# A 32-batch attention stage: a reordered step, maxima negated in the reduction, queries two batches ahead, and key transfers issued before stores

## The chip, the core and the metric

The kernel runs as one program on one core of a Trainium2 chip. The core has five instruction queues that run side by side and meet only through semaphores: TensorE (PE: matmuls and transposes), VectorE (DVE), ScalarE (ACT), GpSimd (POOL) and SyncE (SP, which here only issues DMA transfers). SBUF is the on-chip memory with 128 partitions; PSUM is the memory that TensorE writes. The metric is the device time of one execution in microseconds (us). The kernel before takes 1517.27 us (median of 3 runs, 1517.0 to 1519.42).

## What is computed

Two transformer layers on x of 32 batches x 128 tokens x 256 features. The change touches only the first piece, a cross attention with 16 heads of 16 features and the layer norm behind it:

```python
def _mha(q, k, v, mask):
    qh = q.reshape(B, S, H, hd).transpose(0, 2, 1, 3)      # kh, vh alike
    scores = jnp.einsum('bhqd,bhkd->bhqk', qh, kh) / jnp.sqrt(jnp.float32(hd))
    scores = scores + mask[:, None, :, :].astype(scores.dtype) * NEG_INF
    probs = jax.nn.softmax(scores, axis=-1)
    out = jnp.einsum('bhqk,bhkd->bhqd', probs, vh)
    return out.transpose(0, 2, 1, 3).reshape(B, S, D)

x1 = x + _mha(layernorm(x), ctx, ctx, mask)
y = layernorm(x1)      # goes into a quantised feed-forward network, then a
                       # second attention and a mixture of 8 experts
```

## The kernel before, in words

`attention0` (lines 44 to 687) runs stage A, the attention above; `feed_forward0` and later functions follow behind a barrier and are not touched. Stage A has no scheduler: every engine's queue is written out by hand as a function `step`, called once for each batch b = 0 to 31 and a few times more to drain. Some calls are unrolled, the middle ones stand in a hardware loop (`Fori`) of four steps; `inside(b, first, last)` leaves out what does not exist at the ends. An engine runs its queue strictly in order, so the order in `step` decides who waits for whom.

For one batch the work is: POOL subtracts the mean and multiplies by the inverse deviation (`queries`, L320 and L323). PE transposes the result (`turn_qy`, L434) and it is scaled out of PSUM into `qT` (`copy_qy`, L639). PE writes mask times -10000 into the score banks (`masks`, L382) and adds the 16 heads' scores (`scores`, L392). The scores fill `ps_score`, four PSUM banks in two halves of 8 heads, and there is only one such tile: the masks of the next batch can go into half 0 only when its exponentials have been read, into half 1 only when DVE's subtraction has read it. DVE takes the row maxima of each half (`maximum`, L507). For half 0 it negates them (`negate`, L511) and ACT uses them as the bias of eight exponentials (`shifted_exponentials`, L619); for half 1 DVE subtracts them itself (`subtract`, L516) and ACT does one exponential over all 8 heads (`exponentials`, L625). PE transposes the probabilities in four quarters through two PSUM buffers (`transposes`, L403), ACT copies each quarter out (`copy_probT`, L631), PE multiplies with the values (`weighted`, L414), ACT copies the sum out (`copy_out`, L648), PE turns it back (`turn_out`, L421), and DVE divides by the sums of the exponentials (`divide`, L522 and L524). POOL adds the result to x (`residual`, L329). DVE takes the statistics (`deviation`, L531), POOL the inverse deviation, DVE normalises and takes the largest absolute value (`normalise`, L540, L543), PE transposes y in the same PSUM tile as the queries (L438), and it is copied to `yT` (L642). DVE also takes the statistics of the batch four ahead (`statistics_ahead`, L571).

SP's `step` waits until x1 of batch b is ready, stores it (L247), and in every second step loads the keys of a pair of batches as 8 transfers (`load_keys`, L214) into one of two slots. In the first step it also issues the last mask chunk (L227), three quarters of the values (`load_v`, L222) and b1T (L261), and late in the stage three groups of weights (`load_w2`, L253).

## Time and profile before

| | |
|---|---|
| runs (3) | 1517.27 us median, 1517.0 to 1519.42 |
| the profiled execution | 1516.37 us, its span 1514.6 us |
| mean granted TensorE clock | 0.954 |
| PE / DVE / ACT / POOL busy, whole span | 89% / 74% / 69% / 25% |
| stage A ends (barrier) | at 292.16 us |
| its busy time in stage A, of 292.16 us | PE 226.69, DVE 212.92, ACT 200.86, POOL 126.72 us |

All later times are from the profiled execution, in us from its span's start. "T of step b" is when DVE begins the first `maximum` of batch b. A start-to-start distance between two neighbouring instructions of an engine is what the first occupies of it; the durations shown are a little longer, since neighbours overlap.

### The profile page before, as it was taken

To read this page: it belongs to the slowest core of one execution; us is meant where nothing else is said; L and a number is where in the kernel's file an instruction comes from. 1 tells how busy PE (TensorE), PEld (TensorE's weight loads), DVE (VectorE), ACT (ScalarE), POOL (GpSimd) and SP (SyncE) were. 2 spreads that over 40 slices of the span, in tenths; PEclk is the share of its full clock that TensorE was granted. 3 is DMA by queue.
4 is the path that set the end of the run, shared out by engine and by line. 5 is a ranking of instruction groups with operands and counts; after the bars stand their busy time and mean duration, and the time that the engine had idled before them with its cause. 6 is when DMAs were issued, how large, how long until landed. Compare 5 with 4: busy or idle time off the path is not lost. (4 is left out here: it accounts for less than half of the span.)

```text
span 1514.6 us, 34646 instructions
## 1 busy us (share of the span) xinstructions
PE 1352.3 (89%) x11261; PEld 1158.5 (76%) x11261; DVE 1126.2 (74%) x1948; ACT 1045.4 (69%) x2717; POOL 374.6 (25%) x639
## 2 busy tenths in 40 slices
PE   5788888899899989997799999899998759999996
PEld 3555555587787768797688888888887649999996
DVE  6677778797858887276577777777776468888895
ACT  4677777566559976562578777777777328888885
POOL 5344444200001111002011111111111124445543
PEclk9999999999899999999799999999999769999999
DMA  7411034448037889733413324233331057211110
GB/s 222 126 35 32 28 101 135 141 163 295 28 125 250 261 289 292 255 112 107 165 64 130 100 79 130 80 101 123 94 135 36 22 196 281 99 55 51 55 43 10
DMA packets 102058, 191.02 MB, mean 126 GB/s; under 512 B 12948, under 2 KB 68145, under 8 KB 95540
## 3 DMA queue, kind: packets, MB, share of 16 engines
q1 hardware_dynamic: 91572, 155.80, 30.5%
q0 software_dynamic: 10176, 33.57, 7.5%
q8 instruction: 67, 1.10, 0.3%
q14 instruction: 51, 0.42, 0.1%
q10 hardware_dynamic: 192, 0.13, 0.0%
HBM read 124.17 MB, written 68.03 MB: 127 GB/s over the span
## 5 line engine op out<-in xcount | busy, mean ns | idle before, releaser
L2040 ACT ACTIVATE c_w_raw<-c_ps_score,c_neg_max 128x128 f32<-128x128 f32 x512 | 182.9, 387 | 51.7 <-DVE c_neg_max L1900 50.9
L2413 PE MATMUL d_ps_hT<-d_zT,d_w_tile 128*128 128x128 f32 x1248 | 147.2, 277 | 2.5 <-DVE d_zT L2520 2.5
L2413 PEld LDWEIGHTS d_ps_hT<-d_zT,d_w_tile 128*128 128x128 f32 x1248 | 144.0, 193 | 3.2 <-DVE d_zT L2520 3.2
L2426 PE MATMUL d_ps_y<-d_w_parts,d_hT 128*128 128x256 f32 x936 | 120.3, 284 | 1.8 <-DVE d_res L2551 1.8
L631 ACT ACTIVATE a_probT<-a_ps_probT 128x512 f32<-128x512 f32 x128 | 71.1, 622 | 68.2 <-PE a_ps_probT L403 68.0
L2586 ACT ACTIVATE d_h<-d_ps_hT,d_b1T 128x128 f32<-128x128 f32 x312 | 88.5, 366 | 41.4 <-PE d_ps_hT L2413 41.4
L2040 ACT ACTIVATION_READ_ACCUMULATOR c_w_raw<-c_ps_score,c_neg_max 128x1 f32 x512 | 116.0, 227 | 0.0
L2426 PEld LDWEIGHTS d_ps_y<-d_w_parts,d_hT 128*128 128x128 f32 x936 | 113.2, 189 | 2.1 <-DVE d_res L2551 2.0
L507 DVE TENSOR_REDUCE a_row_max<-a_ps_score 128x8 f32<-128x1024 f32 x64 | 78.0, 1219 | 44.9 <-PE a_ps_score L392 44.9
L1777 PE MATMUL c_ps_proj<-c_xnT,c_wq 128*128 128x256 f32 x768 | 110.0, 296 | 0.0
L1825 PE MATMUL c_ps_aux<-c_wo,c_attnT 128*128 128x256 f32 x768 | 105.1, 296 | 0.0
L2539 DVE TENSOR_TENSOR d_w_parts<-d_w,d_w_parts 128x1024 fp32r<-128x1024 f32 x78 | 95.3, 1221 | 12.0 <-ACT d_w_parts L2598 12.0
L1777 PEld LDWEIGHTS c_ps_proj<-c_xnT,c_wq 128*128 128x128 f32 x768 | 98.5, 198 | 5.0 <-issue 4.8
L1825 PEld LDWEIGHTS c_ps_aux<-c_wo,c_attnT 128*128 128x128 f32 x768 | 98.4, 198 | 4.3 <-issue 0.4
L1900 DVE TENSOR_REDUCE c_neg_max<-c_ps_score 128x4 f32<-128x512 f32 x128 | 82.5, 686 | 22.5 <-PE c_ps_score L1747 22.5
L1907 DVE TENSOR_TENSOR c_w_raw<-c_w_raw,c_inv_sum 128x512 f32<-128x512 f32 x128 | 88.9, 694 | 4.4
L2598 ACT ACTIVATE d_w_parts<-d_w 128x1024 fp32r x78 | 81.9, 1051 | 10.0 <-PE d_ps_y L2426 10.0
L1144 ACT ACTIVATE b_act<-b_ps 128x512 f32<-128x512 f32 (+1 forms) x96 | 54.5, 603 | 49.7 <-PE b_ps L1039 42.4
L1088 PE MATMUL b_ps<-b_w_parts,b_ctx_high 128*128 128x512 f32 x256 | 82.4, 403 | 4.3 <-DMA b_ctx_low<-split_scratch 4.3
L1078 PE MATMUL b_ps<-b_ctx_high,b_w_parts 128*128 128x512 f32 x256 | 82.5, 397 | 2.8 <-ACT b_out L1207 2.7
L619 ACT ACTIVATE a_prob<-a_ps_score,a_shift 128x128 f32<-128x128 f32 x256 | 75.1, 409 | 11.5 <-DVE a_shift L511 10.4
L1722 POOL TENSOR_TENSOR c_var_o<-c_mv_o,c_eps 128x1 f32<-128x1 f32 x32 | 6.1, 190 | 307.8 <-DVE c_mv_o L1941 307.8
(307 smaller groups left out, 3527.9 us busy)
## 6 DMA issues: line engine op xcount, KB each, us to landing
keys_scratch<-b_out SPq DMA_DIRECT2D x64, 256.0 KB, 3.2
values_scratch<-b_out SPq DMA_DIRECT2D x64, 256.0 KB, 3.9
c_kT<-keys_scratch SPq DMA_DIRECT2D x16, 1024.0 KB, 6.4
d_w<-w_in SPq DMA_DIRECT2D x16, 1024.0 KB, 7.5
split_scratch<-b_split SPq DMA_DIRECT2D x12, 1024.0 KB, 4.7
c_v_more<-values_scratch SPq DMA_DIRECT2D x24, 512.0 KB, 4.1
a_w<-w_in SPq DMA_DIRECT2D x64, 128.0 KB, 2.6
b_ctx_high<-split_scratch POOLq DMA_DIRECT2D x16, 512.0 KB, 5.3
```

The source lines that it names most:

```text
L1078: last = pe.matmul(ps[:, bank(n), :], w_parts[:, h, a, k, column:column + P], ctx_parts[c % 2][b][:, k, :], start=(j == 0), stop=(j == ND ...
L1088: last = pe.matmul(ps[:, bank(n), :], ctx_parts[c % 2][a][:, k, t * P:(t + 1) * P], w_parts[:, h, b, k, :], start=(j == 0), stop=(j == ND ...
L1777: last = pe.matmul(ps_proj[:, j, h * PT:(h + 1) * PT], weights[:, a, k, blk * P:(blk + 1) * P], src[:, c, k, :], start=(n == 0), stop=(n = ...
L1825: last = pe.matmul(ps_aux[:, 0:D], attnT[:, s, a, blk, :], wo[:, c, blk, :], start=False, stop=(n == BLKS * len(PARTS) - 1))
L1900: dve.tensor_reduce(neg_max[:, n, :], ps_score[:, n % 2], AX_X, ALU.max, negate=True).then_inc(max_done, 1)
L1907: dve.tensor_tensor(prob[:, n], prob[:, n], inv_sum[:, n, :].unsqueeze(2).to_broadcast([P, HB, P]), ALU.mult).then_inc(prob_ready, 1)
L2040: last = act.activation(prob[:, n, j, :], ps_score[:, n % 2, j, :], ACT.Exp, bias=neg_max[:, n, j:j + 1], accum_out=row_sum[:, n, j:j + 1])
L2413: last = pe.matmul(ps_hT[:, f, :], w1_tile[:, half, k, n * P:(n + 1) * P], zT[:, s, k, :], start=(k == 0), stop=(k == ND - 1))
L2426: last = pe.matmul(ps_y[:, 0:D], hT[:, s, a, f, :], w2_parts[:, half, b, n, :], start=(f == 0 and (a, b) == PARTS[0]), stop=(f == FB - 1 a ...
L2539: dve.tensor_tensor(w2_parts[:, half, 1], w2[:, e, half * FB // 2:(half + 1) * FB // 2, :], w2_parts[:, half, 0].bitcast(F32), ALU.subtrac ...
L2586: act.activation(h[:, f, :], ps_hT[:, f, :], ACT.Relu, bias=b1T[:, e, f:f + 1]).then_inc(h_ready, 1)
L2598: act.activation(w2_parts[:, half, 0], w2[:, e, half * FB // 2:(half + 1) * FB // 2, :], ACT.Copy)\
```

## The change

No piece of arithmetic is dropped except one small instruction. `negate` goes: the reduction of half 0 gets `negate=half == 0`, and the bias of the exponentials is `row_max` itself. The rest is order:

- PE: a step does masks and scores of b, then the second half of the transposes and all of `weighted` of batch b-2, then queries of b+2 (and y), then the first half of the transposes of b-1, and `turn_out` of b-2 last. Before, all four quarters and `weighted` were of b-1, in the step directly behind.
- DVE: both maxima and the subtraction come first, `divide` behind them. In odd steps DVE makes the two copies of `copy_qy`, which ACT made in every step.
- ACT: exponentials first, the copy of `out` between their two groups, the copies of the transposed probabilities last.
- POOL: queries of b+3 instead of b+2, values of b instead of b+1.
- SP: keys are issued when their scores are done, and x1 is stored two steps later, so the wait for x1 no longer stands ahead of them. The values come in step 1 (one quarter) and step 3 (two), the last mask chunk and b1T in step 1. The groups of `w2` go in steps 22, 24 and 30 instead of 21, 23 and 28.

```diff
+                def store_x1(b):
+                    sp.wait_ge(x1_ready, b + 1)
+                    sp.dma_start(x1_dram[b], x_sb[:, b, :]).then_inc(x1_stored, 16)
+
+
+
                 def step(b, u, pair):
                     if u % 2 == 1 and inside(b, 0, NB - 5):
                         sp.wait_ge(scores_done, b + 1)
                         load_keys(pair + 2, u // 2)
-                    sp.wait_ge(x1_ready, b + 1)
-                    sp.dma_start(x1_dram[b], x_sb[:, b, :]).then_inc(x1_stored, 16)
+                    if inside(b, 2, NB + 1):
+                        store_x1(b - 2)
 
...
-                    if b == 0:
+                    if b == 1:
                         load_mask(3)
-                        for c in range(1, 4):
-                            load_v(c)
                         sp.dma_start(b1T[:], b1T_dram).then_inc(b1_loaded, 16)
+                        load_v(1)
+                    if b == 3:
+                        load_v(2)
+                        load_v(3)
...
                 def step(b, u):
                     s = u % 2
-                    if inside(b, 0, NB - 3):
-                        queries(b + 2, s, (u + 2) % UN)
+                    if inside(b, 0, NB - 4):
+                        queries(b + 3, 1 - s, (u + 3) % UN)
                     if inside(b, 2, NB + 1):
                         residual(b - 2, s)
                         inverse_deviation(b - 2, s)
                     if inside(b, 4, NB - 5):
                         deviation_ahead(b, u)
-                    if inside(b, 1, NB - 2):
-                        values(b + 1, 1 - s)
+                    if inside(b, 2, NB - 1):
+                        values(b, s)
 
                 deviations(0, 2, 1)
                 queries(0, 0, 0)
+                queries(1, 1, 1)
                 masks(0)
-                queries(1, 1, 1)
                 deviations(2, 2, 2)
+                queries(2, 0, 2)
                 pool.wait_ge(v_loaded[0], 16)
...
                 def step(b, u):
-                    p, pu = b - 1, (u - 1) % UN
                     if inside(b, 0, NB - 1):
                         if u == 0 and not isinstance(b, int):
                             pe.wait_ge(mask_ready, 4)
                         masks(b)
                         scores(b, u)
+                    if inside(b, 2, NB + 1):
+                        transposes(b - 2, u % 2, 2)
+                        transposes(b - 2, u % 2, 3)
+                        for q in range(NQ):
+                            weighted(b - 2, (u - 2) % UN, q)
+                    turn_qy(b + 2, u % 2)
                     if inside(b, 1, NB):
-                        transposes(p, pu % 2, 0)
-                        transposes(p, pu % 2, 1)
+                        transposes(b - 1, 1 - u % 2, 0)
+                        transposes(b - 1, 1 - u % 2, 1)
                     if isinstance(b, int) and b == NB:
                         turn_weights(0)
                     if inside(b, 2, NB + 1):
                         turn_out(b - 2)
-                    turn_qy(b + 1, (u + 1) % 2)
-                    if inside(b, 1, NB):
-                        transposes(p, pu % 2, 2)
-                        transposes(p, pu % 2, 3)
-                        for q in range(NQ):
-                            weighted(p, pu, q)
 
...
                 def maximum(b, half):
-                    n = 2 * b + half + 1
                     if half == 0:
                         dve.wait_ge(scores_done, b + 1)
-                    dve.tensor_reduce(row_max[:, half, :], ps_score[:, half], AX_X, ALU.max).then_inc(max_done, 1)
-                    dve.wait_ge(max_done, n)
-
-                def negate(b):
-                    dve.tensor_scalar(shift[:], row_max[:, 0, :], -1.0, None, ALU.mult).then_inc(shift_ready, 1)
+                    dve.tensor_reduce(row_max[:, half, :], ps_score[:, half], AX_X, ALU.max, negate=half == 0).then_inc(max_done, 1)
 
                 def subtract(b, s):
+                    dve.wait_ge(max_done, 2 * (b + 1))
                     if inside(b, 2, NB):
                         dve.wait_ge(probT_done, NQ * (b - 1))
                     dve.tensor_tensor(prob[:, s, 1], ps_score[:, 1],
...
+                def copy_qy(g, s):
+                    dve.wait_ge(qy_done, g + 1)
+                    if inside(g, 0, NB - 1):
+                        if inside(g, 2, NB - 1):
+                            dve.wait_ge(scores_done, g - 1)
+                        dve.tensor_scalar(qT[:, s], ps_qy[:, 0], float(HD0) ** -0.5, None, ALU.mult).then_inc(qT_ready, 1)
+                    if inside(g, 6, NB + 5):
+                        dve.tensor_copy(yT[:, :, bass.ds((g - 6) * P, P)], ps_qy[:, 1]).then_inc(yT_ready, 1)
+
                 def step(b, s):
-                    here = inside(b, 0, NB - 1)
-                    if here:
+                    if inside(b, 0, NB - 1):
                         maximum(b, 0)
-                        negate(b)
+                        maximum(b, 1)
+                        subtract(b, s)
+                    if s == 1:
+                        copy_qy(b + 2, s)
                     if inside(b, 2, NB + 1):
                         divide(b - 2, s)
-                    if here:
-                        maximum(b, 1)
-                        subtract(b, s)
                     if inside(b, 3, NB + 2):
                         normalise(b - 3, 1 - s)
                     if inside(b, 2, NB + 1):
...
                 def shifted_exponentials(b, s, q):
                     if q == 0:
-                        act.wait_ge(shift_ready, b + 1)
+                        act.wait_ge(max_done, 2 * b + 1)
                     for h in range(HB * q, HB * (q + 1)):
-                        last = act.activation(prob[:, s, 0, h, :], ps_score[:, 0, h, :], ACT.Exp, bias=shift[:, h:h + 1])
+                        last = act.activation(prob[:, s, 0, h, :], ps_score[:, 0, h, :], ACT.Exp, bias=row_max[:, 0, h:h + 1])
                     if q == 1:
...
                 def step(b, u):
-                    here, back = inside(b, 0, NB - 1), inside(b, 1, NB)
-                    if back:
-                        copy_probT(b - 1, 0)
-                        copy_probT(b - 1, 1)
+                    here = inside(b, 0, NB - 1)
                     if here:
                         shifted_exponentials(b, u % 2, 0)
-                    copy_qy(b + 1, (u + 1) % 2)
-                    if back:
-                        copy_probT(b - 1, 2)
-                        copy_probT(b - 1, 3)
+                    if inside(b, 2, NB + 1):
+                        copy_out(b - 2)
                     if here:
                         shifted_exponentials(b, u % 2, 1)
                         exponentials(b, u % 2)
-                    if back:
-                        copy_out(b - 1)
+                    if u % 2 == 0:
+                        copy_qy(b + 2, 0)
+                    if inside(b, 1, NB):
+                        for q in range(NQ):
+                            copy_probT(b - 1, q)
 
```


What stands in TensorE's queue for one middle step (batch 6), from its masks to its last instruction:

```order
L382 MATMUL a_ps_score<-a_neg_eye,a_mask 128x512 x4
L392 MATMUL a_ps_score<-a_keys,a_qT 128x256 x8
L403 MATMUL a_ps_probT<-ident,a_prob 128x128 x8
L421 MATMUL a_ps_out<-ident,a_outT 128x128 x4
L434 MATMUL a_ps_qy<-ident,a_q_in 128x128 x2
L438 MATMUL a_ps_qy<-ident,a_y 128x128 x2
L403 MATMUL a_ps_probT<-ident,a_prob 128x128 x8
L414 MATMUL a_ps_out<-a_probT,a_v_ones 32x128 x16
```
and with the change:

```order
L389 MATMUL a_ps_score<-a_neg_eye,a_mask 128x512 x4
L399 MATMUL a_ps_score<-a_keys,a_qT 128x256 x8
L410 MATMUL a_ps_probT<-ident,a_prob 128x128 x8
L421 MATMUL a_ps_out<-a_probT,a_v_ones 32x128 x16
L441 MATMUL a_ps_qy<-ident,a_q_in 128x128 x2
L445 MATMUL a_ps_qy<-ident,a_y 128x128 x2
L410 MATMUL a_ps_probT<-ident,a_prob 128x128 x8
L428 MATMUL a_ps_out<-ident,a_outT 128x128 x4
```
The products with the values (`a_ps_out<-a_probT,a_v_ones`) move from the step's end to right behind the first transposes, and the turn of `a_outT` moves to the step's end.

VectorE's queue, an unrolled step before (batch 3):

```order
L507 TENSOR_REDUCE a_row_max<-a_ps_score 128x8
L511 TENSOR_SCALAR a_shift<-a_row_max 128x8
L522 RECIPROCAL a_inv_sum<-a_ps_out 128x16
L524 TENSOR_TENSOR a_attn<-a_ps_out,a_inv_sum 128x256
L507 TENSOR_REDUCE a_row_max<-a_ps_score 128x8
L516 TENSOR_TENSOR a_prob<-a_ps_score,a_row_max 128x1024
L540 TENSOR_SCALAR a_y<-a_x,a_mv,a_rstd 128x256
L543 TENSOR_REDUCE ymax<-a_y 128x1
L531 BN_STATS a_stats<-a_x 128x6
L534 BN_AGGR a_mv<-a_stats 128x2
```
and with the change, an unrolled odd step (batch 5):

```order
L513 TENSOR_REDUCE a_row_max<-a_ps_score 128x8 x2
L519 TENSOR_TENSOR a_prob<-a_ps_score,a_row_max 128x1024
L555 TENSOR_SCALAR a_qT<-a_ps_qy 128x256
L557 COPY yT<-a_ps_qy 128x2x128
L525 RECIPROCAL a_inv_sum<-a_ps_out 128x16
L527 TENSOR_TENSOR a_attn<-a_ps_out,a_inv_sum 128x256
L543 TENSOR_SCALAR a_y<-a_x,a_mv,a_rstd 128x256
L546 TENSOR_REDUCE ymax<-a_y 128x1
L534 BN_STATS a_stats<-a_x 128x6
L537 BN_AGGR a_mv<-a_stats 128x2
```
`a_shift` is gone, the reciprocal comes behind the subtraction, and two copies out of `a_ps_qy` have come in ahead of it. Even steps do not have these two.

SyncE's queue at the start, from the last part of x on, before:

```order
L218 DMA a_x<-x_in 128x8x256
L247 DMA x_scratch<-a_x 128x256
L227 DMA a_mask_int<-mask_t_in 128x1024
L222 DMA a_v_raw<-ctx_in 128x8x256 x3
L261 DMA b1T<-b1T_in 128x64
L214 DMA a_keys<-ctx_blocks_in 16x2x256 x8
```
and with the change:

```order
L216 DMA a_x<-x_in 128x8x256
L212 DMA a_keys<-ctx_blocks_in 16x2x256 x8
L225 DMA a_mask_int<-mask_t_in 128x1024
L263 DMA b1T<-b1T_in 128x64
L220 DMA a_v_raw<-ctx_in 128x8x256
L242 DMA x_scratch<-a_x 128x256
L212 DMA a_keys<-ctx_blocks_in 16x2x256 x8
L242 DMA x_scratch<-a_x 128x256
L220 DMA a_v_raw<-ctx_in 128x8x256 x2
```
The 8 key transfers stood behind a store (`x_scratch<-a_x`), a mask chunk, three quarters of the values and b1T; now they stand ahead of all of these.

## Rows read from the trace of the kernel before

**Rows 1.** The windows view: span, busy us (instructions) per engine, granted clock, DMA.

```profile
core 0: us, PE busy (x) PEld busy (x) DVE busy (x) ACT busy (x) POOL busy (x), PEclk, DMA share, GB/s
54.22:85.40 31.18, 26.62 (x305) 18.73 (x306) 25.36 (x48) 24.61 (x64) 13.14 (x29) 0.95 0.12 36
85.40:252.94 167.54, 137.51 (x1521) 90.94 (x1522) 130.00 (x240) 123.37 (x320) 74.39 (x162) 0.93 0.23 69
94.91:102.52 7.61, 6.29 (x77) 4.32 (x77) 6.28 (x13) 6.10 (x16) 2.19 (x6) 1.00 0.11 30
102.52:112.03 9.51, 7.94 (x77) 4.95 (x77) 6.60 (x12) 6.21 (x16) 5.22 (x12) 0.82 0.12 34
252.94:275.37 22.43, 18.94 (x229) 12.99 (x230) 17.09 (x31) 18.34 (x48) 8.07 (x17) 1.00 0.18 47
```
**Rows 2.** Waits in stage A: who waited for whom, us in total, times, longest.

```profile
engine line waited for: us in total, times, longest us
...
DVE a_row_max L507 <- PE a_ps_score L392: 44.9, 31, 4.1
...
PE a_ps_score L392 <- DMA a_keys<-ctx_blocks_in: 6.4, 2, 6.1
```
**Rows 3.** The same view for SyncE's queue in stage A.

```profile
SPq L247 <- POOL a_x L329: 122.6, 25, 9.9
```
**Rows 4.** The timeline of one step at full clock, three engines mixed.

```profile
start us, us, engine line op out<-in xcount [idle before <-releaser]
...
208.28 1.22 ACT L619 ACTIVATE a_prob<-a_ps_score,a_shift 128x128 f32<-128x128 f32 x4
...
209.64 1.03 PE L382 MATMUL a_ps_score<-a_neg_eye,a_mask 128*128 128x512 f16 x4 [0.70 <-ACT a_prob L619]
...
211.82 1.22 DVE L507 TENSOR_REDUCE a_row_max<-a_ps_score 128x8 f32<-128x1024 f32 x1 [0.75 <-PE a_ps_score L392]
...
213.08 0.57 DVE L511 TENSOR_SCALAR a_shift<-a_row_max 128x8 f32<-128x8 f32 x1
...
213.56 0.24 DVE L522 RECIPROCAL a_inv_sum<-a_ps_out 128x16 f32<-128x16 f32 x1
213.68 1.14 ACT L619 ACTIVATE a_prob<-a_ps_score,a_shift 128x128 f32<-128x128 f32 x4
213.84 0.42 DVE L524 TENSOR_TENSOR a_attn<-a_ps_out,a_inv_sum 128x256 f32<-128x256 f32 x1
214.18 1.21 DVE L507 TENSOR_REDUCE a_row_max<-a_ps_score 128x8 f32<-128x1024 f32 x1
214.44 0.73 POOL L329 TENSOR_TENSOR a_x<-a_x,a_attn 128x256 f32 x1 [0.82 <-DVE a_attn L524]
...
214.69 0.40 ACT L639 ACTIVATE a_qT<-a_ps_qy 128x256 f32<-128x256 f32 x1
...
215.52 1.23 DVE L516 TENSOR_TENSOR a_prob<-a_ps_score,a_row_max 128x1024 f32<-128x1024 f32 x1
...
216.66 0.41 DVE L540 TENSOR_SCALAR a_y<-a_x,a_mv,a_rstd 128x256 f32 x1
...
217.54 0.42 DVE L531 BATCH_NORM_STATS2 a_stats<-a_x 128x6 f32 x1
...
218.28 0.43 DVE L571 BATCH_NORM_STATS2 a_stats_next<-a_x 128x6 f32 x1
```
**Rows 5.** The same timeline one step earlier: masks, and the maximum that follows.

```profile
200.41 1.89 PE L382 MATMUL a_ps_score<-a_neg_eye,a_mask 128*128 128x512 f16 x4 [0.70 <-ACT a_prob L619]
...
204.21 1.23 DVE L507 TENSOR_REDUCE a_row_max<-a_ps_score 128x8 f32<-128x1024 f32 x1 [2.31 <-PE a_ps_score L392]
```
**Rows 6.** VectorE's timeline: first maxima of batch 1 and batch 4.

```profile
24.91 1.23 DVE L507 TENSOR_REDUCE a_row_max<-a_ps_score 128x8 f32<-128x1024 f32 x1 [2.40 <-PE a_ps_score L392]
...
54.22 1.23 DVE L507 TENSOR_REDUCE a_row_max<-a_ps_score 128x8 f32<-128x1024 f32 x1 [3.63 <-PE a_ps_score L392]
```
**Rows 7.** SyncE's row for the keys of batches 4 and 5.

```profile
43.80 5.31 SPq L214 DMA_DIRECT2D a_keys<-ctx_blocks_in  x8
```
**Rows 8.** TensorE's row for the scores of batch 4.

```profile
52.07 2.09 PE L392 MATMUL a_ps_score<-a_keys,a_qT 32*128 32x256 f32 x16 [6.06 <-DMA a_keys<-ctx_blocks_in]
```
**Rows 9.** SyncE's row for the first group of w2.

```profile
215.66 11.29 SPq L253 DMA_DIRECT2D a_w<-w_in  x24
```
**Rows 10.** TensorE's row for the turn of batch 31's output.

```profile
285.44 0.66 PE L421 MATMUL a_ps_out<-ident,a_outT 128*128 128x128 f32 x4
```

More of the change, by code:

```diff
@@ L264, in _ @@
                         step(UN * i + u, u, 2 * i + u // 2)
-                for b in range(20, NB):
+                for b in range(20, NB + 2):
                     step(b, b % UN, b // 2)
-                    if b == 21:
+                    if b == 22:
                         sp.wait_ge(x1_stored, 16 * 16)
@@ L434, in turn_qy @@
                             last = pe.transpose(ps_qy[:, 0, k, :], q_in[:, s, k * P:(k + 1) * P], ident[:])
-                    if inside(g, 5, NB + 4):
-                        pe.wait_ge(y_ready, g - 4)
+                    if inside(g, 6, NB + 5):
+                        pe.wait_ge(y_ready, g - 5)
                         for k in range(ND):
-                            last = pe.transpose(ps_qy[:, 1, k, :], y[:, 1 - s, k * P:(k + 1) * P], ident[:])
+                            last = pe.transpose(ps_qy[:, 1, k, :], y[:, s, k * P:(k + 1) * P], ident[:])
                     last.then_inc(qy_done, 1)
                 def step(b, u):
-                    p, pu = b - 1, (u - 1) % UN
                     if inside(b, 0, NB - 1):
@@ L474, in _ @@
                 turn_qy(0, 0)
+                turn_qy(1, 1)
                 pe.wait_ge(mask_ready, 1)
@@ L597, in _ @@
                 statistics(2, 4)
-                for b in range(UN):
+                for b in range(2 * UN):
                     step(b, b % 2)
@@ L601, in _ @@
                         statistics(4, 8)
-                for c in range(2, 5):
-                    dve.wait_ge(x_loaded[c], 16)
-                dve.wait_ge(b1_loaded, 16)
-                dve.tensor_scalar(b1T[:], b1T[:], 0.0, None, ALU.max).then_inc(relu_b1_ready, 1)
-                with dve.Fori(1, NB // UN - 1) as i:
+                    if b == UN - 1:
+                        for c in range(2, 5):
+                            dve.wait_ge(x_loaded[c], 16)
+                    if b >= UN:
+                        statistics_ahead(b, b % UN)
+                with dve.Fori(2, NB // UN - 1) as i:
                     for u in range(UN):
@@ L609, in _ @@
                         statistics_ahead(UN * i + u, u)
-                for b in range(NB - UN, NB + 3):
+                dve.wait_ge(b1_loaded, 16)
+                dve.tensor_scalar(b1T[:], b1T[:], 0.0, None, ALU.max).then_inc(relu_b1_ready, 1)
+                for b in range(NB - UN, NB + 4):
                     step(b, b % 2)
@@ L637, in copy_qy @@
                             act.wait_ge(scores_done, g - 1)
-                        last = act.activation(qT[:, s], ps_qy[:, 0], ACT.Copy, scale=float(HD0) ** -0.5)
-                        last.then_inc(qT_ready, 1)
-                    if inside(g, 5, NB + 4):
-                        act.activation(yT[:, :, bass.ds((g - 5) * P, P)], ps_qy[:, 1], ACT.Copy).then_inc(yT_ready, 1)
+                        act.activation(qT[:, s], ps_qy[:, 0], ACT.Copy, scale=float(HD0) ** -0.5).then_inc(qT_ready, 1)
+                    if inside(g, 6, NB + 5):
+                        act.activation(yT[:, :, bass.ds((g - 6) * P, P)], ps_qy[:, 1], ACT.Copy).then_inc(yT_ready, 1)
                 def copy_out(b):
@@ L672, in _ @@
                 copy_qy(0, 0)
+                copy_qy(1, 1)
                 for b in range(UN):
```

15 lines of the change are left out of this document (7 added, 8 removed).

## The prediction

> **What bounds the kernel now.** I read the windows view first, cut at the first maximum of batches 4, 8, 28 and 31 [rows 1]. Between batch 8 and 28 a step takes 167.54/20 = 8.38 us, and no engine is busy all of it: PE 137.51, DVE 130.00, ACT 123.37 us. So the stage is bound by a loop of waits. The list of waits says who waits: DVE's maxima for PE's scores, 44.9 us in 31 waits [rows 2]. The timeline of one step then gives the loop [rows 4]. From T (211.82, first maximum; the one before is at 204.21 [rows 5], so the step took 7.61) DVE reduces and negates, ACT starts the exponentials at 213.68, four of them occupy 1.01 (to the next at 214.69), other copies come between, and the second four, which stood at 208.28 in the step before, are followed by the masks at 209.64 (1.36 later) and the next maximum at 211.82 (2.18 later). The negation is on this loop, and so are the ACT copies that stand between the two groups of exponentials.
>
> The second thing is the clock. At 200.41 the same four mask matmuls take 1.89 instead of 1.03 us, and the maximum follows 3.80 us after them instead of 2.18 [rows 4, 5]. PE runs there at its 1.2 GHz level. One such step is the window from 102.52: 9.51 us, mean clock 0.82 [rows 1]. Against steps of 7.61 the 20 steps hold 167.54 - 152.2 = 15.3 us of this.
>
> The third is the start: from batch 1's maximum to batch 4's it is 29.31 us [rows 6], and PE stood still 6.06 of these for the keys of batch 4 [rows 8], whose transfers SyncE issued only at 43.80 [rows 7], behind the wait for x1 (SyncE spends 122.6 us of the stage in that wait [rows 3]).
>
> **The change, part by part.**
>
> *ACT and PE's loop.* Without the negation an exponential can start about where the negation did (213.08, 1.26 behind T), say 1.28. Then 1.01 for four exponentials, 0.5 for the copy of `out` (an estimate from ACT's other starts; its row is a 128x512 copy), then 1.36 and 2.18 as above: 1.28 + 1.01 + 0.50 + 1.36 + 2.18 = 6.33 us. The copy of `out` needs the products of batch b-2. PE makes their transposes right behind the scores; two ACT copies and the products end about 2.1 behind T, while DVE still reduces, and the copy is due at 2.29. That is close, 0.2 us.
>
> *DVE's own step.* A full 128x1024 pass occupies 1.14 when an independent instruction follows (215.52 to 216.66) and 1.34 when the follower waits for it (214.18 to 215.52). In the new order: maximum 1.14, maximum 1.34, subtraction 1.14, reciprocal 0.28 (213.56 to 213.84), division 0.34 (to 214.18), normalise and its maximum 0.88 (216.66 to 217.54), statistics 0.74 (to 218.28), and again 0.74 for the four batches ahead: 6.60. POOL's residual starts 0.60 behind the division and takes 0.73, so x1 is there 1.33 behind it, and the statistics would come at 1.22: I add 0.17 with the signal. Even steps: 6.77. Odd steps have two copies out of PSUM more. No row shows them on DVE. The nearest is the division, which reads PSUM in the same 256 elements: 0.42 long, 0.34 occupied. They can't gain DVE anything; they cost nothing where DVE would have waited for `turn_out` anyway, and at most 2 x 0.42. I take 0.68, from the nearest row: odd steps 7.45, mean 7.11 (6.77 to 7.19). No row shows a reduction that negates either; between nothing and the 0.48 that the negation occupies today (213.08 to 213.56) I take nothing, since one pass over PSUM sets its length. DVE is thus the bound, with ACT and PE 0.4 to 1.1 us ahead of it, and no wait of DVE for PE stays in the loop, provided `turn_out` is in time. It needs the copy of `out` (2.29 + 0.7 = 3.0 behind T) and takes 0.66: 3.7, where DVE's reciprocal is due at 3.62. This is the place where I am least sure.
>
> *POOL.* It gets no new work (74.39 of 167.54 us busy [rows 1]). Queries of b+3 and values of b are each made a step ahead of PE's need, so I count nothing; without that cover a late query would hold PE's `turn_qy` by up to its two passes. DVE's small work on b1T moves out of step 3, where it lay beside the wait for keys: nothing.
>
> *The clock.* A low step lengthens the masks-to-maximum stretch by 3.80 - 2.18 = 1.62, and the loop of 6.33 becomes 7.95. That is 0.84 over DVE's 7.11, where it costs 1.88 today. How often it falls can't be read before the run. PE's idle share goes from 17% to about 11% of a step (6.29 busy of 7.61 [rows 1], against 6.29 of 7.11), which speaks for less of it; but the two idle pieces, ahead of `turn_out` and ahead of the masks, stand close together, which speaks for some of it. I take six such steps, 5.0 us; the ends are 0 and 17 (all 20).
> The Trainium skill, page "TensorE: Matmul & The Clock Gate", section "A second HAM failure mode: psum-queue depth-cycling", says that frequent short idle pieces between groups of matmuls are enough to make the clock swing. This trace agrees in kind: the clock is 0.82 in a step in which PE is busy 7.94 of 9.51 us [rows 1]. By that rule fewer pieces mean less swing and the term is nearer 0 than 5. The section "HAM oscillation" of the same page puts it down to long stalls for data; by that alone today's low steps should not be there.
>
> *Sum for the middle.* Batches 8 to 28: 20 x 7.11 + 5.0 = 147.2 against 167.54, 20.3 less. Batches 4 to 8: 4 x 7.11 = 28.4 against 31.18, 2.7 less. Batches 28 to 31 have no statistics ahead: even steps 6.03, held up to the other loop's 6.33, odd 6.71, so 6.33 + 6.71 + 6.33 = 19.4 against 22.43, 3.1 less [rows 1].
>
> *The start.* Keys of batch 4 can be issued when SyncE has issued the last part of x and batch 1's scores are done (its maximum is at 24.91 [rows 6]), about 26 instead of 43.80. Issue takes 5.31, and the scores started 52.07 - 49.11 = 3.0 behind the last issue, so they are there by 35 to 38, ahead of need at 42. Batch 1's maximum comes 0.6 earlier (the negation, and a first half that is not held up). Then three steps without the full load, 6.33 each: 19.0 instead of 29.31. Together 10.9 less. The values, which used to go ahead of the keys, are not needed before batch 8. If the stretch goes at 7 us a step it is 8.9.
>
> *The end.* `turn_out` of batch 31 is at 285.44, 10.07 behind its maximum at 275.37 [rows 1, 10]. In the new order the products of a batch come one step later. With the durations above: ACT has batch 30's first two copies done at 5.9, PE its second transposes at 6.5, ACT the copies at 7.1, PE the products at 7.5, then the first transposes of batch 31, two pieces of weight transposes and the turn of batch 30 to 10.1, the second transposes of batch 31 to 11.0, ACT's copies to 11.7, two weight copies and the copy of `out` to 13.3, and the turn at 13.4. This costs 3.3.
>
> *The weights w2.* 24 issues take 11.29 us [rows 9] and the keys of batch 28 stand behind two groups and those of batch 26. Counted from batch 22's maximum: the store of batch 20 is free at about 5.9, then 11.3 of w2, 5.0 of keys, 0.9 of stores, 11.4 of w2 and 5.0 of keys end at 39.5, and another 1.5 to 3.0 to land. They are needed at 6 x 7.11 less 1.2, at 41.4. I take nothing. If they are late it is 1 to 5 us. The last group ends about 10 us behind batch 31's maximum, and its readers come at 14.6.
>
> *Total.* 20.3 + 2.7 + 3.1 + 10.9 - 3.3 = 33.7 us. The profiled execution took 1516.37, so 1482.7. The median of the runs is 0.9 higher. I say 1483. Nothing behind stage A changes but its starting time.
>
> **The rivals.**
>
> *DVE waits for the turned output (18%).* If the products of b-2 miss the copy of `out` by a little, everything behind shifts: copy, `turn_out`, reciprocal, and DVE's whole rest. A turn 0.5 us later than I think makes all steps about 7.6. For: the margin is 0.1 to 0.2 us. Against: DVE's slower pace lets PE get ahead. Then 31.18 - 30.4 = 0.8, 167.54 - 152 - 5 = 10.5, 3.1, 10.9, -3.3: 22 less, 1494.
>
> *The clock stays up (7%).* Without the low steps 5 us more go: 1478. The Trainium skill's rule on short idle pieces, in the page named above, would have it so.
>
> *Keys late behind w2 (6%).* 1 to 5 us at batch 28, and again a little at 26: 1487.
>
> *Slower: PE falls to the low level and stays (7%).* With products, y and transposes between the scores and the next masks, a PE at 1.2 GHz has a full step of its own. Its 6.3 us of a fast step, stretched as masks were (1.89/1.03), are about 11.3 us, and DVE waits for `turn_out`. The other terms sum to 2.7 + 3.1 + 10.9 - 3.3 = 13.4, so nothing is won when the 20 steps average (167.54 + 13.4)/20 = 9.05: 46% of them low. With 60% low they average 9.6, 192 us, and the kernel is at 1516.4 - 13.4 + 192 - 167.5 = 1528. Against it: a PE that is busy through the step is what brought the clock back each time so far; a low step today is followed by a fast one.
>
> *No change (4%).* Each saving is only idle time moved, and another wait of the old size, 7.6 with today's low steps, takes over: the start's gain is eaten by the end and the weights, 1516. What speaks for it is only that four orders were tied together in one edit.
>
> **How the numbers follow.** My forecast has 58%, own range 1475 to 1490. Faster are the forecast and the first three rivals: 0.89. Within 0.2%, some 3 us and about what a measurement of this kernel can tell from no change: 0.04. Slower: 0.07. The range of 8 in 10 reaches from the best clock, with a DVE step of 7.0, to beyond the first rival: 1474 to 1504.
>
> **What would show it.** Right: the first maxima of batches 8 and 28 are 142 to 149 us apart; even steps are shorter than odd ones by about 0.7; DVE waits less than 10 us for scores in stage A where it was 44.9; no wait of PE for keys at batch 4; stage A ends near 258 instead of 292.16; mean clock in the middle not under 0.93. Wrong: DVE idle ahead of the reciprocal in most steps (first rival), PE idle on keys at batch 26 or 28 (third), clock under 0.8 in the middle (slower), or steps of 7.6 with DVE idle ahead of the maxima, which would mean that ACT and PE's loop is longer than my 6.33.

## The result

The changed kernel takes 1480.14 us (median of 4 runs, 1478.72 to 1482.64), the kernel before 1517.13 us beside it. The ratio is 0.9766, 95% interval 0.974 to 0.9793: 2.3% faster. A second set on another chip gave 1476.95 us and 0.9764 (0.9723 to 0.9806). The profiled execution took 1479.33 us, 37.0 less than the one before. The forecast was 1483, from 33.7 us less.

### The profile page after: what moved, and what is told of

Same layout as the page of the kernel before. It is cut to its first block and busy times, and to the rows that moved or that the text cites. A ratio compares the mean times of both kernels' runs of the same rounds, so it can differ in the third digit from the quotient of the medians.

```text
span 1477.6 us, 34587 instructions
## 1 busy us (share of the span) xinstructions
PE 1343.2 (91%) x11261; PEld 1153.9 (78%) x11261; DVE 1124.8 (76%) x1947; ACT 1038.3 (70%) x2686; POOL 374.7 (25%) x639
## 5 line engine op out<-in xcount | busy, mean ns | idle before, releaser
L634 ACT ACTIVATE a_prob<-a_ps_score,a_row_max 128x128 f32<-128x128 f32 x256 | 73.7, 391 | 23.5 <-DVE a_row_max L513 22.2
L1759 PE MATMUL c_ps_score<-c_kT,c_qT 64*128 64x128 f32 x1024 | 76.6, 290 | 4.5 <-issue 3.0
```

## The profile after

In the windows view of the changed kernel the cuts are again the first maxima of batches 4, 8, 28 and 31, which now stand at 43.10, 71.02, 216.02 and 235.01. The third row is an odd step at the end of a turn of the hardware loop, the fourth an even one:

```profile
core 0: us, PE busy (x) PEld busy (x) DVE busy (x) ACT busy (x) POOL busy (x), PEclk, DMA share, GB/s
43.10:71.02 27.92, 26.20 (x320) 18.17 (x322) 25.35 (x49) 24.02 (x61) 14.99 (x32) 1.00 0.36 114
71.02:216.02 145.00, 128.09 (x1524) 86.62 (x1520) 127.77 (x242) 118.58 (x301) 74.30 (x162) 1.00 0.27 79
150.31:158.17 7.86, 7.37 (x104) 5.01 (x101) 6.77 (x15) 6.68 (x16) 4.08 (x10) 1.00 0.18 50
158.17:165.04 6.87, 5.46 (x55) 3.68 (x52) 6.05 (x11) 5.19 (x15) 3.31 (x7) 1.00 0.06 19
216.02:235.01 18.99, 17.78 (x220) 12.07 (x220) 17.28 (x31) 17.28 (x45) 6.91 (x15) 1.00 0.11 33
```
The first, second and last of these rows answer to [rows 1]: 27.92 us for 31.18, 145.00 for 167.54, 18.99 for 22.43. The mean clock is 1.00 in all of them. VectorE is busy 127.77 of 145.00 us, which is 88%; it was 78%.

Its waits in the stage, from the list of waits (who waited for whom, us in total, times, longest):

```profile
DVE a_stats L534 <- POOL a_x L335: 8.4, 32, 0.9
...
DVE a_inv_sum L525 <- PE a_ps_out L428: 7.0, 5, 5.2
...
DVE a_row_max L513 <- PE a_ps_score L399: 4.2, 4, 2.1
...
DVE a_row_max L513 <- issue: 1.3, 4, 0.4
...
PE a_ps_score L399 <- DMA a_keys<-ctx_blocks_in: 0.5, 1, 0.5
```
VectorE waited 44.9 us for scores before [rows 2]; now 4.2, all in the first batches. Of its waits for the turned output (7.0 us) none lies between batches 8 and 28; 6.1 us of them are in the drain, the last steps of the stage. What stays in the middle is 0.2 to 0.3 us a step for GpSimd's x1, ahead of the statistics, and 0.3 to 0.4 us at each turn of the hardware loop, which the list calls "issue". The wait for keys is 0.5 us instead of 6.4.

The timeline of an even step, batch 20, from its first maximum to the next step's (start, duration, engine, line), answers to [rows 4]:

```profile
158.17 2.35 DVE L513 TENSOR_REDUCE a_row_max<-a_ps_score 128x8 f32<-128x1024 f32 x2 [0.32 <-issue]
...
159.43 1.14 ACT L634 ACTIVATE a_prob<-a_ps_score,a_row_max 128x128 f32<-128x128 f32 x4 [1.19 <-DVE a_row_max L513]
...
160.44 0.61 ACT L661 ACTIVATE a_outT<-a_ps_out 128x512 f32<-128x512 f32 x1
160.66 1.22 DVE L519 TENSOR_TENSOR a_prob<-a_ps_score,a_row_max 128x1024 f32<-128x1024 f32 x1
160.91 1.17 ACT L634 ACTIVATE a_prob<-a_ps_score,a_row_max 128x128 f32<-128x128 f32 x4
...
161.11 0.66 PE L428 MATMUL a_ps_out<-ident,a_outT 128*128 128x128 f32 x4 [0.93 <-ACT a_outT L661]
161.80 0.26 DVE L525 RECIPROCAL a_inv_sum<-a_ps_out 128x16 f32<-128x16 f32 x1
...
162.23 1.03 PE L389 MATMUL a_ps_score<-a_neg_eye,a_mask 128*128 128x512 f16 x4 [0.46 <-ACT a_prob L634]
...
163.19 1.15 PE L399 MATMUL a_ps_score<-a_keys,a_qT 32*128 32x256 f32 x16
...
163.66 0.43 DVE L534 BATCH_NORM_STATS2 a_stats<-a_x 128x6 f32 x1 [0.26 <-POOL a_x L335]
...
164.41 0.43 DVE L583 BATCH_NORM_STATS2 a_stats_next<-a_x 128x6 f32 x1
...
165.04 2.32 DVE L513 TENSOR_REDUCE a_row_max<-a_ps_score 128x8 f32<-128x1024 f32 x2
```
The exponentials start 1.26 us behind the maximum, where they started 1.86 behind it, because no negation and no copy of transposed probabilities is ahead of them. The copy of `out` starts at 2.27, the second exponentials at 2.74, the masks at 4.06. VectorE takes up the reciprocal at 3.63 without a wait. Its next maximum, at 165.04, has no idle time ahead of it, while the scores began at 163.19 and were there some 0.6 us earlier. VectorE's own queue sets the step.

Term by term, from the two profiled executions:

| | forecast, less | measured, less |
|---|---|---|
| start, to batch 4's maximum | 10.9 | 54.22 - 43.10 = 11.1 |
| batches 4 to 8 | 2.7 | 31.18 - 27.92 = 3.3 |
| batches 8 to 28 | 20.3 | 167.54 - 145.00 = 22.5 |
| batches 28 to 31 | 3.1 | 22.43 - 18.99 = 3.4 |
| from there to the stage's end | -3.3 | 16.79 - 21.34 = -4.55 |
| everything behind stage A | 0 | 1.2 |
| sum | 33.7 | 37.0 |

Stage A ended at 292.16 and ends at 256.35.

## Experiments

All ratios are to the kernel before, run on the same chip; stage times are from each run's own profile.

**1. The negation alone, in the old order.**

```diff
# shortened: the semaphores are left out
-    dve.tensor_reduce(row_max[:, half, :], ps_score[:, half], AX_X, ALU.max)
+    dve.tensor_reduce(row_max[:, half, :], ps_score[:, half], AX_X, ALU.max, negate=half == 0)
-    negate(b)                                   # and bias=row_max instead of shift
```

> The kernel before with one part of the change: the maxima of half 0 are negated in the reduction, the separate negation is gone, all orders as before. Theory (the negation stands on the loop of waits, 0.5 to 0.6 us a step): full-clock steps fall from 7.61 to about 7.05, DVE (6.69 occupied) still waits a little for scores; over 31 steps 15 us less if the low clock falls as often as before, 1502. If a busier TensorE alone keeps the clock up, another 5 to 13 us go: 1490 to 1497. Rival (the new order alone makes the gain): the exponentials start earlier but the copies between them hold the loop, steps stay near 7.6, 1513 to 1517.

1504.75 us, ratio 0.9934 (0.9909 to 0.9959). From batch 7 to 25 the steps are 7.63 us, all at full clock, neither the 7.05 nor the "near 7.6 with nothing won" that I had set against each other. Its timeline tells why (one step):

```profile
145.87 1.23 DVE L507 TENSOR_REDUCE a_row_max<-a_ps_score 128x8 f32<-128x1024 f32 x1 [0.76 <-PE a_ps_score L392]
...
146.50 1.08 ACT L628 ACTIVATE a_probT<-a_ps_probT 128x512 f32<-128x512 f32 x2 [1.52 <-PE a_ps_probT L403]
...
147.47 1.15 ACT L616 ACTIVATE a_prob<-a_ps_score,a_row_max 128x128 f32<-128x128 f32 x4
...
149.96 1.22 ACT L616 ACTIVATE a_prob<-a_ps_score,a_row_max 128x128 f32<-128x128 f32 x4
...
151.32 1.03 PE L382 MATMUL a_ps_score<-a_neg_eye,a_mask 128*128 128x512 f16 x4 [0.70 <-ACT a_prob L616]
...
153.50 1.23 DVE L507 TENSOR_REDUCE a_row_max<-a_ps_score 128x8 f32<-128x1024 f32 x1 [0.75 <-PE a_ps_score L392]
```
The maximum ends at 147.10, but the exponentials start at 147.47, 1.60 behind its start: ScalarE is still in two copies of transposed probabilities, which it could begin only at 146.50. So in the old order the negation was worth 0.25 to 0.3 us of a full-clock step (7.87 to 7.92 before, 7.63 now), not its 0.5, and the copies were the next wait, 0.3 us behind it. What more was won came from the clock: batches 8 to 28 take 156.25 us instead of 167.54, and between 57 and 238 us no stretch is low. The run lost some again at the tail, where TensorE waited 2.3 us for keys behind w2, in a step of 10.9 us.

Even these 0.3 us are not the negation's own work. In the kernel before it takes 0.17 us in the step of batch 22 and 0.57 in that of batch 23. The POOL row ahead of each is the second of GpSimd's two passes over the queries:

```profile
203.82 0.61 POOL L323 TENSOR_TENSOR a_q_in<-a_q_in,a_rstd_next 128x256 f32<-128x256 f32 x1
...
204.21 1.23 DVE L507 TENSOR_REDUCE a_row_max<-a_ps_score 128x8 f32<-128x1024 f32 x1 [2.31 <-PE a_ps_score L392]
...
205.47 0.17 DVE L511 TENSOR_SCALAR a_shift<-a_row_max 128x8 f32<-128x8 f32 x1
...
205.80 1.14 ACT L619 ACTIVATE a_prob<-a_ps_score,a_shift 128x128 f32<-128x128 f32 x4
...
213.01 0.61 POOL L323 TENSOR_TENSOR a_q_in<-a_q_in,a_rstd_next 128x256 f32<-128x256 f32 x1
213.08 0.57 DVE L511 TENSOR_SCALAR a_shift<-a_row_max 128x8 f32<-128x8 f32 x1
```
At 213.08 the pass is running, and the negation ends 0.03 us behind it (213.65 and 213.62). At 205.47 it was over long before, and the exponentials start 1.59 us behind the maximum, as they do without a negation (1.60). In the traces of the kernel before and of experiments 2 and 6 the negation takes over 0.18 us 42 times, and each time it ends 0.02 to 0.03 us behind an instruction of GpSimd that had begun first. Where no such instruction had more than 0.12 us to go, it took 0.17 us. What the old order paid for was this meeting; a negation of 0.17 us would have hidden behind the copies.

**2. SyncE's part alone.** The new order of SyncE's queue (diff above), all else as before.

> The kernel before with SyncE's part of the change alone: keys ahead of stores, stores two steps later, values in steps 1 and 3, w2 one or two steps later. Theory (only the start waits for keys): TensorE's 6.06 us wait at batch 4 goes, batch 4's maximum comes near 47.5 instead of 54.2, steps stay 7.61 and 9.5; 1510 to 1511. Rival (stores and keys collide later, or w2 comes late): a wait for keys at batch 26 or 28 of 1 to 5 us, 1512 to 1516.

1506.02 us, ratio 0.9942 (0.9919 to 0.9965). Batch 4's maximum is at 47.59 instead of 54.22, 6.6 earlier, as expected, and the steps are as slow as before: 167.1 us for batches 8 to 28, clock 0.93. No wait of TensorE for keys is left in the stage.

**3. The new step without SyncE's part.** SyncE's queue as in the kernel before, everything else as changed.

> The changed kernel with SyncE's old order (stores of x1 ahead of keys, values in step 0). Theory A (SyncE's part and the other part add up): the start's 6.6 us come back and nothing else, 1487. Theory B (the faster, deeper step needs the new SyncE order): x1 of a batch is ready later in its step now, so keys issued behind its store land about when a step needs them or later; waits of TensorE for keys in most pairs of batches, 0.5 to 2 us each, 1492 to 1500.

1516.8 us, ratio 1.0013 (0.9992 to 1.0034): without SyncE's part nothing is left, not even the 0.0066 that the negation alone gave (experiment 1), which this kernel has too. It is theory B, with more than I gave it. The waits of TensorE in its stage A, and the scores of batch 4:

```profile
engine line waited for: us in total, times, longest us
...
PE a_ps_score L391 <- DMA a_keys<-ctx_blocks_in: 35.9, 14, 10.2
```
```profile
51.14 2.09 PE L391 MATMUL a_ps_score<-a_keys,a_qT 32*128 32x256 f32 x16 [10.16 <-DMA a_keys<-ctx_blocks_in]
```
35.9 us of waits for keys in 14 steps, where the kernel before had 6.4 in 2 [rows 2]. At batch 4 the wait is 10.16 us against 6.06 [rows 8], because the steps ahead of it are shorter and the transfers are not. Batches 8 to 28 take 164.2 us. The keys of batch 18, in the kernel before and in this one:

```profile
153.82 1.23 DVE L507 TENSOR_REDUCE a_row_max<-a_ps_score 128x8 f32<-128x1024 f32 x1 [0.75 <-PE a_ps_score L392]
...
157.97 5.84 SPq L214 DMA_DIRECT2D a_keys<-ctx_blocks_in  x8
...
168.40 1.15 PE L392 MATMUL a_ps_score<-a_keys,a_qT 32*128 32x256 f32 x16
```
```profile
151.81 2.36 DVE L505 TENSOR_REDUCE a_row_max<-a_ps_score 128x8 f32<-128x1024 f32 x2 [0.48 <-PE a_ps_score L391]
...
158.39 5.83 SPq L212 DMA_DIRECT2D a_keys<-ctx_blocks_in  x8
...
165.88 1.15 PE L391 MATMUL a_ps_score<-a_keys,a_qT 32*128 32x256 f32 x16 [1.62 <-DMA a_keys<-ctx_blocks_in]
```
Both issue them behind the store of x1. Before, that was 4.15 us behind the first maximum of batch 16, and the last of the 8 transfers landed 3.1 us ahead of the scores. Here x1 is ready later in the step, because `divide` has moved behind the subtraction (its reciprocal starts 4.13 us behind the maximum instead of 1.73), so the issue comes at 6.58 us. The next two steps are shorter too, and the scores wait for the landing. In the changed kernel, with SyncE's new order, the same keys are issued 8.3 us ahead of that maximum. The waits are not all of the loss: in batches 16 to 24, where no stretch is low, a step takes 7.65 us against 7.26 in the changed kernel, and the rest is longer waits behind w2 (up to 5.0 us) and low clock (0.94 in batches 8 to 28 against 1.00).

**4. Both, in the old order.** Negation and SyncE's part; PE, ACT, DVE and POOL in their old order.

> The kernel before with the negated maxima and SyncE's part, but the old order of all other engines: everything except the new step. Theory (the new step itself is worth what steps of 6.87 to 7.47 save against 7.63, and the rest adds up): start as in the run with SyncE's part alone (batch 4's maximum near 47.3), steps 7.63 at full clock, batches 8 to 28 in 153 us with no wait for keys, stage A ends near 270, 1496; so the step's order is worth some 16 us on top. Rival (with SyncE free the old order with negation is as fast as the new one): steps under 7.4, 1482 to 1488.

1494.1 us, ratio 0.9844 (0.9802 to 0.9886). Batches 8 to 28 take 152.4 us, steps of 7.62, no wait for keys, and the stage ends at 268.21. The changed kernel ends it at 256.35, in the second profile at 254.65. So the new order of the four engines is worth 12 to 14 us, given the other two parts (I expected some 16). Without SyncE's part it costs: 1.0013 with it (experiment 3) against 0.9934 without (experiment 1), both with the negation gone. The negation's and SyncE's parts themselves add up: 0.9934 x 0.9942 = 0.9877, and 0.9844 (0.9802 to 0.9886) was measured.

**5. The two copies: all on ScalarE, all on VectorE.** In the changed kernel VectorE makes them in odd steps.

```diff
# shortened
-    if s == 1:                      # DVE
-        copy_qy(b + 2, s)
-    if u % 2 == 0:                  # ACT
-        copy_qy(b + 2, 0)
+    copy_qy(b + 2, u % 2)           # ACT, every step; the other run: DVE, every step
```

> The changed kernel with both copies out of the query PSUM tile on ScalarE in every step, none on VectorE. Theory (VectorE's own queue is the bound of the step): odd steps lose the 0.62 us by which they are longer than even ones, steps 6.87, batches 8 to 28 in 139 us instead of 145, 1473. Rival (the loop of ScalarE and TensorE is as long as VectorE's step): the copies delay the transposed probabilities and the exponentials, odd steps stay near 7.4, 1479 to 1483.

> The changed kernel with both copies on VectorE in every step. Theory (VectorE is the bound): even steps become as long as odd ones, +0.62 us in some 15 steps, batches 8 to 28 in 151 us, 1489. Rival (another loop is the bound and VectorE has room in even steps): 1480 to 1483.

All on ScalarE: 1474.09 us, ratio 0.9734 (0.9706 to 0.9762). All on VectorE: 1484.55 us, 0.9817 (0.9792 to 0.9843). The windows of batches 8 to 28, first all on ScalarE, then all on VectorE:

```profile
69.49:209.24 139.75, 126.94 (x1518) 86.24 (x1516) 121.59 (x222) 124.42 (x320) 75.49 (x164) 1.00 0.27 82
```
```profile
71.14:223.56 152.42, 129.87 (x1544) 87.08 (x1536) 134.23 (x261) 113.88 (x282) 74.60 (x162) 1.00 0.25 75
```
139.75, 145.00 and 152.42 us for 0, 10 and 20 steps with the copies on VectorE. That is a straight answer on the bound: each pair of copies costs the step 0.5 to 0.75 us, and ScalarE takes them for nothing. A second set of the ScalarE version gave 0.973 (0.9696 to 0.9763):

> The changed kernel with all copies of the query tile on ScalarE, once more and in more rounds, for its interval against the kernel before: ratio 0.973 to 0.974, 1473 to 1475; batches 8 to 28 in 139.8 us.

The profile had 139.6 us again, but the median on that chip was 1478.88, beside 1519.05 for the kernel before: only ratios compare between chips.

**6. The negation apart, in the new order.**

> The changed kernel with the negation as an instruction of its own again, between the two maxima. Theory (in the new order VectorE's queue is the bound and every instruction in it costs): the first maximum occupies 0.20 more and the negation 0.15 or more, exponentials start 0.5 us later, the turned output comes about 0.2 us after VectorE could use it; steps 7.25 to 7.7, batches 8 to 28 in 154 us, 1489. Rival (the negation hides as it did in the old order, where taking it out gave 0.25 us a step): 1482 to 1485.

1491.09 us, ratio 0.9857 (0.9822 to 0.9891). Batches 8 to 28 take 150.5 us instead of 145.0, 0.27 a step; I expected 0.45. Batch 4's maximum is 2.5 us later, but that is the clock: this profile has a second low stretch there (27.83 to 31.24), and one and the same program (experiment 5, all on ScalarE) had that maximum at 42.60 in one profile and at 44.70 in the other. The negation costs about as much a step as in the old order, but by another way: there by GpSimd's pass in the loop of waits, here by VectorE's queue, where it takes 0.17 us in most steps and the first maximum occupies 1.23 us instead of 1.11.

**7. What keeps the clock up.** One reduction more in VectorE's step, over 512 or 1024 columns of the idle weight tile.

> The changed kernel with one more VectorE reduction in every step, over 128x512 of the idle weight tile, which nothing reads. Looked at for the clock. VectorE's step becomes 7.25 + 0.60 = 7.85 us, batches 8 to 28 157 us. Theory (what keeps TensorE's clock up is how much of the step it is busy): TensorE is busy 80% of the step as in the kernel before, low stretches come back in batches 8 to 28, mean clock 0.93 to 0.98. Rival (the new order, which spreads the products with the values and the turns through the step, keeps it up): clock 1.00 there. The loop with low clock is some 8 us, so the time itself changes little with it.

> The same with 128x1024, twice the work. VectorE's step becomes 7.25 + 1.14 = 8.4 us, batches 8 to 28 168 us, TensorE busy 75% of it. Theory (busy share): more low stretches than with 512, mean clock in batches 8 to 28 under 0.95. Rival (order): clock 1.00.

Batches 8 to 28, first 512, then 1024 columns more:

```profile
74.92:229.58 154.66, 129.70 (x1536) 86.72 (x1528) 137.35 (x262) 119.04 (x301) 75.04 (x161) 1.00 0.25 74
```
```profile
75.82:242.08 166.26, 136.50 (x1531) 90.88 (x1532) 148.31 (x262) 118.37 (x300) 74.79 (x161) 0.95 0.23 70
```
The first took 154.66 us with the clock at 1.00 (1490.61 us, one run), the second 166.26 us with 0.95 (1507.54 us, one run) and four low stretches, one of them twice as long as the others. So the new order does not keep the clock up by itself; with longer steps it falls as before. And the old order keeps it up when its steps are shorter (experiments 1 and 4, 7.62 to 7.63 us, clock 1.00). Order alone is ruled out as the cause: at a step of 7.62 us both orders keep the clock at 1.00 (experiment 4, and all copies on VectorE in experiment 5). Whether it plays a part is open, since no run has the new order at the 7.9 us at which the old one falls. That TensorE stands idle for less of the step fits both orders. But the run with 512 was expected to show low stretches and did not (its step was 7.73 us and not 7.85), so how the clock depends on the step stays open.

**8. The drain.** Copies on ScalarE, and in batch 31's step:

```diff
# shortened; the first two lines tell the new order in words
+    # ACT, b == 31: copy_probT(30, 0), copy_probT(30, 1), exponentials(31),
+    # copy_qy(33), copy_probT(30, 2), copy_probT(30, 3)
-    copy_weights(0), copy_weights(1)   # in step 32
+    copy_weights(0), copy_weights(1)   # in step 33, behind copy_out(31)
```

> All copies of the query tile on ScalarE, as in the run of that kind, and in the drain two things more: in batch 31's step ScalarE copies two quarters of batch 30's transposed probabilities ahead of its last exponential, and the copies of the transposed weights come behind the last copy of the output. Theory: batches 8 to 28 in 139.8 us, and TensorE's 1.9 us wait for the first copy after batch 31's scores falls under 1; from batch 31's maximum to the end of the stage 20.0 us instead of 21.3 to 21.8; 1472 to 1473. Rival (TensorE waits for something else in the drain): the same 21.3 to 21.8, 1474.

> The changed kernel itself, on the same chip as the next one, to compare the two: 1478 to 1482, batches 8 to 28 in 145 us.

1473.61 us, ratio 0.9739 (0.9705 to 0.9773). TensorE's wait for the first copy falls to 0.95 us, with a new one of 0.46 behind it; it was 1.90 in the changed kernel and 2.17 in the ScalarE version of experiment 5. From batch 31's maximum to the stage's end it takes 19.65 us. But the changed kernel itself, in the run beside it, took 19.94, and its first profile 21.34. The difference between those two is a low stretch of 3.4 us in the drain, which the first had and the second not. The two profiles of experiment 5's ScalarE version took 21.83 and 21.86, each with a low stretch there too; less the same 1.4 us (an estimate) they are at 20.4. So the drain edit is worth 0.3 to 0.8 us, and most of what I had meant to mend was the clock.

Both ScalarE versions (with the old drain and with the new) end stage A earlier than the changed kernel: 250.45, 252.39 and 249.06 against 256.35 and 254.65. For the whole kernel the intervals overlap (0.973 to 0.974 against 0.976), since the stages behind took 1224 to 1225 us in these profiles against 1218 to 1221, with the same code. All copies on ScalarE is likely the best version, by some 4 us, but that is shown for the stage alone.

## Why the prediction was right, point by point

The bound was right, its size too to 0.14 us a step, and every gain and loss in the table has the sign that was forecast. That the sum came within 3.3 us is in part luck: in batches 8 to 28 the clock gave 5.0 us more than forecast and the turns of the hardware loop took 2.8 back, and in the drain a low stretch of 1.4 us was in this profile and not in the second. The signs named ahead came: 145.00 us between the first maxima of batches 8 and 28, even steps 0.6 us shorter than odd ones, 4.2 us of waits for scores, no wait for keys at batch 4, the stage's end at 256.35, clock 1.00 in the middle.

**The bound.** Right. VectorE's queue sets the step; experiment 5 moved the bound both ways by moving its load. The working was right to 0.1 us: an odd step takes 7.47 (7.45 forecast), an even one 6.82 to 6.89 (6.77). Missing was a fixed piece at the end of each turn of VectorE's hardware loop: the fourth, odd step takes 7.86 to 7.92. The mean is thus 7.25 instead of 7.11. The kernel before could not show it, since there VectorE waited for scores in every step. The copies out of PSUM are 0.41 long on VectorE, as the nearest row had said.

**The loop of ACT and PE.** The forecast placed the exponentials, the copy, the second exponentials and the masks at 1.28, 2.29, 2.79 and 4.15 behind the maximum; they are at 1.26, 2.27, 2.74 and 4.06. The first rival did not come, but by little: TensorE turns the output at 2.94 in place of 3.0, in 0.66 us, so that it is done at 3.60, and VectorE takes up the reciprocal at 3.63. In odd steps VectorE makes its two copies in between and the margin is wide.

**The steps before: one reading was wrong.** I took 7.61 as the step at full clock and called everything above it, 15.3 us, the price of low clock. Experiment 1 led back to the trace: where no stretch is low, the first maxima stand at 161.69, 169.62 and 177.54, 7.9 us apart. In the middle a step of 7.61 comes only behind a low one, when GpSimd is done with the queries before the negation begins and the negation takes 0.17 instead of 0.57 to 0.62 (experiment 1). Two undisturbed steps:

```profile
161.69 1.23 DVE L507 TENSOR_REDUCE a_row_max<-a_ps_score 128x8 f32<-128x1024 f32 x1 [0.69 <-PE a_ps_score L392]
162.95 0.62 DVE L511 TENSOR_SCALAR a_shift<-a_row_max 128x8 f32<-128x8 f32 x1
...
169.62 1.23 DVE L507 TENSOR_REDUCE a_row_max<-a_ps_score 128x8 f32<-128x1024 f32 x1 [0.69 <-PE a_ps_score L392]
```
So the undisturbed step was 7.9, and low clock cost 167.54 - 158 = 9.5 us, in 7 of the 20 steps. The total did not suffer, because it was taken against 167.54. Of the two terms the shorter step is the larger one: 158 - 145 = 13 us.

**The clock.** Mis-sized: 5.0 us forecast for low steps, 0 measured in batches 8 to 28, which is the second rival's case (7%). The loop's end took part of it back: 20 x (7.25 - 7.11) = 2.8 us the other way. The Trainium skill, page "TensorE: Matmul & The Clock Gate", section "A second HAM failure mode: psum-queue depth-cycling", put the swing down to frequent short idle pieces. By that rule the term was to be nearer 0 than 5, and the trace has 0. But the number of the pieces does not tell the kernels apart: TensorE has 2.05 idle pieces over 0.1 us a step before (clock 0.93) and 2.00 in experiment 4 (1.00), and in experiment 7 it is 2.00 with 512 columns (1.00) and 1.80 with 1024 (0.95). So the term came out as the rule has it, but no run here shows that the pieces' number is the reason; why the clock stayed up is open.

**The start.** 11.1 for 10.9. SyncE issued the keys at 25.70, and batch 4's scores did not wait. A match this close is chance in part: batch 4's maximum lies between 42.4 and 45.6 us in the traces with the new order of all engines, SyncE's included, with low clock in different places around batch 1.

**The keys behind w2.** Taken as nothing, and 0.5 us was measured, one wait, which cost VectorE nothing: the step from batch 27 to 28 takes 7.65 us, and 7.66 in the kernel of experiment 5 that has no such wait. The margin is thin: with steps of 6.9 (all copies on ScalarE, experiments 5 and 8) TensorE waits 1.8 us there and the same step takes 7.96 to 8.01 us.

**The drain.** -3.3 forecast, -4.55 measured; without a low stretch -3.15 (19.94 against 16.79). The last turn was forecast 13.4 us behind batch 31's maximum; it is at 13.6 without the low stretch and at 15.0 with it. The order costs what was worked out, and the clock the rest.

**What I had not seen:** that the two halves of the edit don't add. In the forecast SyncE's part was worth the start alone, and the keys' later position in a step was never worked out for the old queue. Experiment 3 (the new order and the negation) gives 1.0013 and experiment 2 (SyncE's part) 0.9942. If the two added up the whole would be 0.9955; it is 0.9766.

## What to carry to other kernels

When a loop of waits is shortened, look for the next thing that arrives: here it was 0.3 us behind the negation, two copies on ScalarE that stood ahead of the exponentials, and a store's wait in the transfer queue. In the old order the keys behind it landed 3 to 4 us early in the middle; in the new one they were late and took the whole gain (experiment 3). Move transfers ahead of waits that belong to other data before making the step shorter. Once an engine's own queue is the bound, its load is worth microseconds and its neighbour's is free: give the copies to the engine that still waits. And before a step is called undisturbed, look at its neighbours: 7.61 us was the step behind a low one, 7.9 the one that repeats itself.

## What the runs showed of the hardware that I had not expected

- A tiny VectorE instruction (the negation, 128x8) took 0.17 us, or up to 0.83 when an instruction of GpSimd was running as it began: 42 times of 42 it then ended 0.02 to 0.03 us behind that one. In a full queue it took 0.17 as well (experiment 6).
- A reduction that negates its result costs nothing: in the changed kernel the 32 negated maxima average 1.20 us and the 32 others 1.21; before, the 64 averaged 1.22.
- The turn of VectorE's hardware loop cost 0.4 us (7.86 to 7.92 against 7.47), in a queue that had no wait there.
- The stages behind stage A, the same code in every kernel here, took 1217 to 1227 us between profiles, which is 0.8% and more than the last experiments were looking for.
